# FFN row transposes one slot later, with their splits, the back transposes, the additions, the store and the next row load

## Chip, cores and metric

The kernel runs on one core of a Trainium2 chip. The metric is device time in microseconds (us) of that core, lower is better. Before the change the median of three runs is 2927.73 us (2926.43 to 2928.63).

## What is computed

One layer of a network on `x` of 16 x 1024 rows of 256 float32 numbers: a graph attention block with its residual, then a feed-forward block (FFN) of eight experts with its residual. The change touches only the FFN:

```python
x = x + _L0_gnn_ref(_layernorm(x), adj, W, a)
x = x + _L0_ffn_ref(_layernorm(x), Wr, br, W1, b1, ..., Wo, bo)

def _L0_ffn_ref(x, ...):
    w = softmax(mean(x, axis=0) @ Wr + br)
    h = relu(bn(einsum('bfd,edh->bfeh', x, W1) + b1))
    h = relu(bn(einsum('bfeh,ehk->bfek', h, W2) + b2))
    y = einsum('bfeh,ehd->bfed', h, Wo) + bo
    return einsum('bfed,fe->bfd', y, w)
```

The gate `w` weighs the eight experts for each of the 1024 row places, from the mean over the 16 batches.

## The kernel before

The attention stage fills the first 715 us or so of the span and is not touched. The FFN stage (`ffn_block`) works on 32 tiles of 512 rows. Each tile goes through eight experts, so there are 256 steps. The work of all engines is written out by hand as one loop of slots: in slot `u` each engine does its part for several steps at once, and `tile_due(u, at, ahead)` says that a once-per-tile job is due in the slot whose place in the tile is `at` (0 to 7), for the tile `ahead` of the current one. "Slot 3" below means a slot with `u % 8 == 3`. Engines run their queues in order and meet at semaphores only.

Per slot, in the order of each queue:

- TensorE (`slot`, from L1040): the layer 2 products of step u+2 (12 matmuls of 512 columns, `z_layer(1, ...)`, read `h1_hi`, `h1_lo`, shown as `z_ps<-h_hi`); then the once-per-tile transposes; then the output products of step u (`y_layer`, 21 matmuls of 256 columns into `m_ps`, L1019 to L1022); then the layer 1 products of step u+4 (12 matmuls, shown as `z_ps<-xT_hi`). Every float32 product is made of three matmuls (`split_matmul`, L52 to L54) from an upper and a lower part of each operand.
- ScalarE (from L1173): second half of a layer 1 activation, two halves of the layer 2 activation of step u+2, upper part `h1_hi` (L1185), first half of the next layer 1 activation (all activations are L1149), the once-per-tile upper parts `xT_hi` (L1124), the upper part `h2_hi` of the layer 2 sums (L1163), and in slot 0 the normalised rows `xn` of the next tile (`normalise`, L1131, four instructions).
- VectorE (from L1259): once-per-tile work first, then the lower part `h2_lo` (L1287), the gating multiply (L1294), the lower part `h1_lo` (L1299), three sums (L1304, L1307, L1310).
- SyncE issues DMAs: the operand `wo_ops` of the next step, once per tile the store of finished rows and the load of rows two tiles ahead, and the gate row. GpSimd finishes the row statistics in slot 6.

The three PSUM banks of `z_ps` are shared: the first layer 1 product of a slot writes the bank that the second half of the layer 2 product of the same slot used, so it waits for ScalarE to have read that (`relu2_ready`). Layer 2 products wait for `h1_lo`.

Once per tile, before the change: slot 0 ScalarE normalises the next tile; slots 1 and 2 TensorE transposes its rows (`transpose_x`, L994, four transposes into the one bank `turn_ps`) and ScalarE takes the upper parts; slots 2 and 3 VectorE takes the lower parts `xT_lo` (`lower_x`, L1227); slots 3 and 4 TensorE transposes the previous tile's output back (`transpose_y`, L1002, same bank); slots 4 and 5 VectorE adds that to the rows (`add_out`, L1232) and adds the bias table to the next tile's rows (`residual`, L1239); slot 6 SyncE stores the rows, VectorE starts statistics (L73). The transposed rows are first read in slot 4, by the layer 1 products at the end of TensorE's slot.

Of the kernel before, what the change touches and what calls it, by code (L numbers as in the profile page):

```python
# [37 lines left out]
def wait(eng, sem, value):  # L38

    if isinstance(value, int) and value <= 0:  # L40
        return
    eng.wait_ge(sem, value)


def bits(ap):

    return ap.bitcast(FP32)
# [749 lines left out]
def ffn_block(nc, B, Wo, x1_dram, w_dram, wo_dram, out, ident, minus_half, node_table, w12_hi, w12_lo,  # L797
# [20 lines left out]
    with ctx:  # L818
# [54 lines left out]
        def is_step(s):  # L873
            return 0 <= s < NS

        def tile_due(u, at, ahead):

            t = u // E + ahead
            return t if u % E == at and 0 <= t < TILES else None
# [3 lines left out]
        @block.sync  # L883
        def _(sp):
            def load_sums(e):
                for m in range(KB):
                    sp.dma_start(wo_sums[e % 2][:, (1 - m):4:2, :],
                                 Wo[e].rearrange("(k p) d -> p k d", p=P)[:, :, m * P:(m + 1) * P]) \
                        .then_inc(sums_in[e % 2], DMA)

            def load_gate(s):
                sp.dma_start(gate[s % 2][:, :], w_dram[s % E, (s // E) % CH].partition_broadcast(P)) \
                    .then_inc(gate_in[s % 2], DMA)

            def load_x1(t):
                sp.dma_start(x1_sb[t % XB][:, :, :], x1_dram[t % CH, t // CH]).then_inc(x1_in[t % XB], DMA)

            def rows_out(t):
                return out[t // CH].rearrange("(c s p) d -> c p s d", c=CH, p=P)[t % CH]

            def slot(u):
                e = u + 1
                if 0 <= e < E:

                    sp.wait_ge(S["wo_lo_ready"], e + 1)
                    sp.dma_start(wo_dram[e], bits(wo_ops[e % 2][:, :, :, :])).then_inc(ops_stored[e % 2], DMA)
                    if e + 2 < E:
                        load_sums(e + 2)
                s = u + 1
                if E <= s < NS:  # L910

                    sp.wait_ge(S["step_done"], s - 1)
                    if s < E + 2:
                        sp.wait_ge(ops_stored[s % 2], DMA * (E // 2))
                    sp.dma_start(bits(wo_ops[s % 2][:, :, :, :]), wo_dram[s % E]).then_inc(ops_in[s % 2], DMA)
                t = tile_due(u, 6, -1)
                if t is not None:
                    sp.wait_ge(S["out_ready"], 2 * (t + 1))
                    sp.dma_start(rows_out(t), x1_sb[t % XB][:, :, :]).then_inc(stored[t % XB], DMA)
                t = tile_due(u, 0, 2)  # L920
                if t is not None:
                    wait(sp, stored[t % XB], DMA * (t // XB))
                    load_x1(t)
                s = u + Z2 + 2
                if u >= -Z2 and s < NS:

                    sp.wait_ge(S["gated_ready"], s - 1)
                    load_gate(s)

            for e in range(2):  # L930
                load_sums(e)
            load_x1(1)
            sp.wait_ge(S["wT_ready"], 1)
            sp.dma_start(w_dram.rearrange("e c n -> e (c n)"), wT_sb).then_inc(w_stored, DMA)
            sp.wait_ge(w_stored, DMA)
            for s in range(2):
                load_gate(s)
            for u in range(-Z1, NS):
                slot(u)
            t = TILES - 1  # L940
            for i, h in enumerate((1, 0)):
                rows = slice(h * CT // 2, (h + 1) * CT // 2)
                sp.wait_ge(S["out_ready"], 2 * t + (i + 1))
                sp.dma_start(rows_out(t)[:, rows, :], x1_sb[t % XB][:, rows, :]).then_inc(stored[t % XB], DMA)
            for i in range(XB):
                sp.wait_ge(stored[i], DMA * (TILES // XB + (1 if i == t % XB else 0)))
            for i in range(2):
                sp.wait_ge(ops_stored[i], DMA * (E // 2))
# [41 lines left out]
        def _(pe):  # L990
# [49 lines left out]
            def slot(u):  # L1040
                s = u + Z2
                if is_step(s):
                    pe.wait_ge(S["h1_lo_ready"], s + 1)
                    wait(pe, S["relu2_ready"], 2 * s - 1)
                    z_layer(1, s % E, 0, h1_hi[s % 2], h1_lo[s % 2])

                    if is_step(s + 1):
                        pe.wait_ge(S["h1_ready"], 2 * (s + 1) + 1)
                    else:
                        pe.wait_ge(S["relu2_ready"], 2 * s)  # L1050
                    z_layer(1, s % E, 1, h1_hi[s % 2], h1_lo[s % 2])
                if u == -2:
                    transpose_gate()
                if u == -1:
                    gate_bias()
                for d in range(KB):
                    t = tile_due(u, 1 + d, 1)
                    if t is not None and u >= 0:
                        pe.wait_ge(norm.xn_ready, t + 1)
                        if d == 0:  # L1060
                            wait(pe, S["out_ready"], 2 * (t - 2))
                        else:
                            pe.wait_ge(S["xT_lo_ready"], 2 * t + 1)
                        transpose_x(turn, d)
                for h in range(2):
                    t = tile_due(u, 3 + h, -1)
                    if t is not None:
                        pe.wait_ge(S["comb_ready"], COMBINES * (t + 1))
                        if h == 0:
                            wait(pe, S["xT_lo_ready"], 2 * min(t + 3, TILES))  # L1070
                        else:
                            pe.wait_ge(S["out_ready"], 2 * t + 1)
                        transpose_y(turn, h)
                s = u
                if is_step(s):
                    pe.wait_ge(S["h2_lo_ready"], s + 1)
                    if s < E:
                        pe.wait_ge(S["wo_lo_ready"], s + 1)
                    else:
                        pe.wait_ge(ops_in[s % 2], DMA * (s // 2 - E // 2 + 1))  # L1080
                    if s == 0:
                        pe.wait_ge(S["table_ready"], 1)
                    elif s % E == 0:
                        pe.wait_ge(S["prod_ready"], 2 * (s // E))
                    y_layer(s % E, wo_ops[s % 2], h2_hi[s % 2], h2_lo[s % 2])
                s = u + Z1
                if is_step(s):
                    i = (s // E) % 2
                    if s % E == 0:
                        pe.wait_ge(S["xT_lo_ready"], 2 * (s // E + 1))  # L1090
                    wait(pe, S["relu2_ready"], 2 * (s - 1))
                    wait(pe, S["h1_ready"], 2 * (s - 1) + 1)
                    z_layer(0, s % E, 0, xT_hi[i], xT_lo[i])
                    wait(pe, S["h1_ready"], 2 * s)
                    z_layer(0, s % E, 1, xT_hi[i], xT_lo[i])
# [17 lines left out]
            for u in range(1 - Z1, NS):  # L1113
                slot(u)
# [6 lines left out]
        def _(act):  # L1121
# [51 lines left out]
            def slot(u):  # L1173
# [17 lines left out]
                t = tile_due(u, E - 1, 0)  # L1191
# [3 lines left out]
                    act.activation(prod[:, 0:4, :].rearrange("p q c -> p (q c)"),  # L1195
                                   m_ps[:, 0:2, :].rearrange("p k c -> p (k c)"), ACT.Copy).then_inc(S["prod_ready"], 1)
                for d in range(KB):
                    t = tile_due(u, 1 + d, 1)
                    if t is not None and u >= 0:
                        upper_x(turn, t, d)  # L1200
                second_upper(u + Z2)
                t = tile_due(u, 0, 1)
# [17 lines left out]
            for u in range(1 - Z1, NS):  # L1220
                slot(u)

        @block.vector
        def _(dve):
# [34 lines left out]
            def slot(u):  # L1259
# [6 lines left out]
                for i in range(2):  # L1266
                    t = tile_due(u, i, -1)
                    if t is not None:
                        combine(t, i)
                    t = tile_due(u, 2 + i, 1)  # L1270
                    if t is not None and u >= 0:
                        lower_x(turn, t, i)
                    t = tile_due(u, 4 + i, -1)
                    if t is not None:
                        dve.wait_ge(S["out_psum"], 2 * t + (i + 1))
                        add_out(turn, t, i)
                    t = tile_due(u, 4 + i, 1)
                    if t is not None and u >= 0:
                        residual(t, i)
                t = tile_due(u, 6, 2)  # L1280
# [31 lines left out]
                t = tile_due(u, 6, 2)  # L1312
                if t is not None:
                    norm.mean_var(dve, t + 1, False)
                t = tile_due(u, E - 1, 0)
# [40 lines left out]
            t = TILES - 1  # L1356
# [44 lines left out]
```

## Time and profile before

| | value |
|---|---|
| median of 3 runs | 2927.73 us |
| profiled execution | 2927.11 us |
| its span, first to last instruction | 2925.3 us |
| mean granted TensorE clock | 0.993 of full |
| TensorE matmul busy | 2812.7 us (96%) |
| VectorE busy | 2414.9 us (83%) |
| ScalarE busy | 2141.2 us (73%) |
| HBM traffic over the span | 151 GB/s |

The span leaves 1.8 us of the profiled execution outside it. Busy time is an average over the whole program; ends of matmuls are modelled, so TensorE's gaps are best read from the starts of instructions.

### The profile page before, as it was taken

What the parts mean: (1) busy time and instruction counts of PE and PEld (TensorE: products, weight loads), DVE (VectorE), ACT (ScalarE), POOL (GpSimd) and SP (SyncE); (2) the same over time, 40 slices, a digit from 0 to 9 for tenths busy, and PEclk for the clock granted to TensorE, in tenths of its full rate; (3) what the DMA queues carried; (4) which work ended last, traced back from release to release, by engine and by line L of the source; (5) the groups of instructions that cost most, each with busy time, mean ns of one, the idle gap of its engine ahead of it and who ended that gap; (6) DMA issues with size and microseconds to landing.
All of it is one profiled execution on the core that took longest, in us unless ns stands there. A gap on an engine that the chain in (4) does not pass through costs nothing.

```text
span 2925.3 us, 48929 instructions
## 1 busy us (share of the span) xinstructions
PE 2812.7 (96%) x17110; PEld 2478.9 (85%) x17110; DVE 2414.9 (83%) x3528; ACT 2141.2 (73%) x3035; POOL 703.6 (24%) x985
## 2 busy tenths in 40 slices
PE   7999999998889999999999999999999999999998
PEld 7989899998678888888888888888888888888887
DVE  7999999996678888888888888888888888888887
ACT  6889888887666676677776676677677777677665
POOL 5888888887100000000000000000000000000000
PEclk9999999999999999999999999999999999999999
DMA  4444444442445455545455445455455445445544
GB/s 145 155 158 152 151 158 151 148 154 93 124 147 156 151 165 159 150 164 160 146 159 160 150 156 160 147 165 160 153 160 160 148 157 161 152 153 161 150 156 136
DMA packets 159980, 445.25 MB, mean 152 GB/s; under 512 B 16016, under 2 KB 73784, under 8 KB 159808
## 3 DMA queue, kind: packets, MB, share of 16 engines
q1 hardware_dynamic: 159808, 442.96, 48.5%
q8 instruction: 108, 1.77, 0.2%
q14 instruction: 64, 0.52, 0.1%
HBM read 401.97 MB, written 40.93 MB: 151 GB/s over the span
## 4 chain that ended last, share of the span: by engine, by line
PE 70%; ACT 3%; DVE 2%; issue 1%; DMA 0%; ACTq 0%; DVEq 0%
PE z_ps L52 16%; PE z_ps L53 16%; PE z_ps L54 16%; PE m_ps L1019 7%; PE m_ps L1021 7%; PE m_ps L1022 7%; ACT ffn_xn L1131 2%; PE turn_ps L994 1%; PE turn_ps L1002 1%; DVE h_lo L1287 1%; DVE h_sums L1294 0%; DVE h_lo L1299 0%; ACT wo_ops L1170 0%; ACT h_hi L1163 0%; PE m_ps L1036 0%
## 5 line engine op out<-in xcount | busy, mean ns | idle before, releaser
L1149 ACT ACTIVATE h<-z_ps,bn_shift,bn_scale 128x512 f32<-128x512 f32 x1024 | 755.7, 775 | 615.0 <-PE z_ps L54 580.3
L1287 DVE TENSOR_TENSOR h_lo<-h_sums,h_hi 128x1792 fp32r<-128x1792 f32 x256 | 518.5, 2026 | 205.6 <-ACT h_hi L1163 202.4
L1019 PE MATMUL m_ps<-h_hi,wo_ops 128*128 128x256 f32 x1792 | 514.5, 287 | 4.0 <-DVE h_lo L1287 4.0
L1022 PE MATMUL m_ps<-h_hi,wo_ops 128*128 128x256 f32 x1792 | 503.9, 281 | 0.0
L1021 PE MATMUL m_ps<-h_lo,wo_ops 128*128 128x256 f32 x1792 | 503.6, 281 | 0.0
L1163 ACT ACTIVATE h_hi<-h_sums 128x1792 fp32r<-128x1792 f32 x256 | 435.4, 1701 | 43.7 <-DVE h_sums L1310 34.0
L86 POOL TENSOR_TENSOR ffn_vareps<-ffn_mv,ln_eps 128x4 f32<-128x4 f32 x32 | 6.4, 199 | 1888.5 <-DVE ffn_mv L80 1888.5
L1294 DVE TENSOR_TENSOR h_sums<-h,gate_row 128x1024 f32<-128x1024 f32 x256 | 313.8, 1226 | 146.9 <-ACT h L1149 127.0
L52 PE MATMUL z_ps<-h_hi,w_hi 128*128 128x512 f32 x1024 | 406.4, 397 | 12.0 <-DVE h_lo L1299 12.0
L52 PE MATMUL z_ps<-xT_hi,w_hi 128*128 128x512 f32 x1024 | 406.6, 397 | 2.3 <-ACT h L1149 1.4
L53 PE MATMUL z_ps<-xT_lo,w_hi 128*128 128x512 f32 x1024 | 405.5, 396 | 0.0
L53 PE MATMUL z_ps<-h_lo,w_hi 128*128 128x512 f32 x1024 | 405.4, 396 | 0.0
L54 PE MATMUL z_ps<-xT_hi,w_lo 128*128 128x512 f32 x1024 | 405.4, 396 | 0.0
L54 PE MATMUL z_ps<-h_hi,w_lo 128*128 128x512 f32 x1024 | 404.8, 395 | 0.0
L1019 PEld LDWEIGHTS m_ps<-h_hi,wo_ops 128*128 128x128 f32 x1792 | 339.4, 189 | 9.9 <-DVE h_lo L1287 4.2
L1021 PEld LDWEIGHTS m_ps<-h_lo,wo_ops 128*128 128x128 f32 x1792 | 339.4, 189 | 5.5
L1022 PEld LDWEIGHTS m_ps<-h_hi,wo_ops 128*128 128x128 f32 x1792 | 338.7, 189 | 0.0
L1299 DVE TENSOR_TENSOR h_lo<-h,h_hi 128x1024 fp32r<-128x1024 f32 x256 | 312.1, 1219 | 1.0 <-ACT h_hi L1185 1.0
L52 PE MATMUL attn_ps<-wh_hi,pT_hi 128*128 128x256 f32 x1024 | 306.5, 299 | 0.0
L53 PE MATMUL attn_ps<-wh_lo,pT_hi 128*128 128x256 f32 x1024 | 289.7, 283 | 0.0
L54 PE MATMUL attn_ps<-wh_hi,pT_lo 128*128 128x256 f32 x1024 | 289.6, 283 | 0.0
L1185 ACT ACTIVATE h_hi<-h 128x1024 fp32r<-128x1024 f32 x256 | 270.3, 1056 | 0.0
(149 smaller groups left out, 5485.4 us busy)
## 6 DMA issues: line engine op xcount, KB each, us to landing
wo_ops<-wo_scratch SPq DMA_DIRECT2D x248, 896.0 KB, 6.4
adj_sb<-in_adj SPq DMA_DIRECT2D x128, 512.0 KB, 3.5
gate_row<-w_scratch SPq DMA_DIRECT2D x256, 256.0 KB, 4.6
x_sb<-in_x SPq DMA_DIRECT2D x64, 256.0 KB, 2.8
x_scratch<-x_sb SPq DMA_DIRECT2D x128, 128.0 KB, 1.8
ffn_x<-x_scratch SPq DMA_DIRECT2D x32, 512.0 KB, 7.8
out<-ffn_x SPq DMA_DIRECT2D x31, 512.0 KB, 8.0
wo_scratch<-wo_ops SPq DMA_DIRECT2D x8, 896.0 KB, 4.2
```

The lines of the kernel that those rows point to most:

```text
L52: pe.matmul(out, w_hi, x_hi, start=first, stop=False)
L53: pe.matmul(out, w_hi, x_lo, start=False, stop=False)
L54: return pe.matmul(out, w_lo, x_hi, start=False, stop=last)
L1019: pe.matmul(m_at(q), w_hi, x_hi[:, x, :], start=e == 0 and q in OPENERS, stop=False, skip_group_check=True)
L1021: pe.matmul(m_at(q), w_hi, x_lo[:, x, :], start=False, stop=False, skip_group_check=True)
L1022: done = pe.matmul(m_at(q), w_lo, x_hi[:, x, :], start=False, stop=e == E - 1, skip_group_check=True)
L1149: return act.activation(dst, src, ACT.Relu, bias=bn_shift[layer][:, col], scale=bn_scale[layer][:, col])
L1163: act.activation(h2_hi[s % 2][:, :, :], g2[:, 1:8, :], ACT.Copy).then_inc(S["h2_hi_ready"], 1)
L1185: act.activation(h1_hi[s % 2][:, :, :], h1[:, :, :], ACT.Copy).then_inc(S["h1_hi_ready"], 1)
L1287: dve.tensor_tensor(h2_lo[s % 2][:, :, :], g2[:, 1:8, :], bits(h2_hi[s % 2][:, :, :]), ALU.subtract) \
L1294: dve.tensor_tensor(h2_rows, h2[:, :, :], gate[s % 2][:, :].unsqueeze(1).to_broadcast([P, KB, BANK]), ALU.mult).then_inc(S["gated_ready"], 1)
L1299: dve.tensor_tensor(h1_lo[s % 2][:, :, :], h1[:, :, :], bits(h1_hi[s % 2][:, :, :]), ALU.subtract) \
```

## The change

Ten once-per-tile jobs get another slot. The two groups of row transposes go from slots 1 and 2 to 2 and 3, with ScalarE's upper parts; VectorE's lower parts from 2 and 3 to 3 and 4; the back transposes from 3 and 4 to 4 and 5; the additions of the output from 4 and 5 to 5 and 6; the store from 6 to 7; the load of the rows two tiles ahead from 0 to 1. The addition of the bias table goes the other way, from slots 4 and 5 to 2 and 3. No instruction is added or removed, and every semaphore wait keeps its value. Slot 0's normalisation, slot 6's statistics and the copies of the products in slot 7 stay.

```diff
@@ SyncE, slot @@
-                t = tile_due(u, 6, -1)
+                t = tile_due(u, 7, -1)
                 if t is not None:
                     sp.wait_ge(S["out_ready"], 2 * (t + 1))
                     sp.dma_start(rows_out(t), x1_sb[t % XB][:, :, :]).then_inc(stored[t % XB], DMA)
-                t = tile_due(u, 0, 2)
+                t = tile_due(u, 1, 2)
@@ TensorE, slot @@
                 for d in range(KB):
-                    t = tile_due(u, 1 + d, 1)
+                    t = tile_due(u, 2 + d, 1)
...
                 for h in range(2):
-                    t = tile_due(u, 3 + h, -1)
+                    t = tile_due(u, 4 + h, -1)
@@ ScalarE, slot @@
                 for d in range(KB):
-                    t = tile_due(u, 1 + d, 1)
+                    t = tile_due(u, 2 + d, 1)
                     if t is not None and u >= 0:
                         upper_x(turn, t, d)
@@ VectorE, slot @@
-                    t = tile_due(u, 2 + i, 1)
+                    t = tile_due(u, 3 + i, 1)
                     if t is not None and u >= 0:
                         lower_x(turn, t, i)
-                    t = tile_due(u, 4 + i, -1)
+                    t = tile_due(u, 5 + i, -1)
                     if t is not None:
                         dve.wait_ge(S["out_psum"], 2 * t + (i + 1))
                         add_out(turn, t, i)
-                    t = tile_due(u, 4 + i, 1)
+                    t = tile_due(u, 2 + i, 1)
                     if t is not None and u >= 0:
                         residual(t, i)
```

## Rows read from the trace of the kernel before

**Rows 1.** The page: TensorE's busy time, share of the span, instructions

```profile
PE 2812.7 (96%) x17110; PEld 2478.9 (85%) x17110; DVE 2414.9 (83%) x3528; ACT 2141.2 (73%) x3035; POOL 703.6 (24%) x985
```

**Rows 2.** TensorE's waits in the whole span: us in total, times, longest

```profile
PE turn_ps L994 <- ACT ffn_xn L1131: 31.0, 31, 2.3
...
PE z_ps L52 <- DVE h_lo L1299: 12.0, 8, 6.3
```

**Rows 3.** Busy time in one stretch: length, engines, granted clock, DMA share, GB/s

```profile
1000.00:1500.00 500.00, 493.34 (x2789) 425.37 (x2788) 409.87 (x497) 351.33 (x407) 24.22 (x35) 1.00 0.50 156
```

**Rows 4.** TensorE in time, slots 0 to 4: start, duration, engine, line, [idle before]

```profile
1782.83 0.39 PE L52 MATMUL z_ps<-h_hi,w_hi 128*128 128x512 f32 x1
...
1790.89 0.39 PE L52 MATMUL z_ps<-h_hi,w_hi 128*128 128x512 f32 x1
...
1794.75 0.66 PE L994 MATMUL turn_ps<-ident,ffn_xn 128*128 128x128 f32 x4 [0.90 <-ACT ffn_xn L1131]
...
1797.71 0.39 PE L52 MATMUL z_ps<-xT_hi,w_hi 128*128 128x512 f32 x1
...
1800.51 0.39 PE L52 MATMUL z_ps<-h_hi,w_hi 128*128 128x512 f32 x1
...
1809.01 0.39 PE L52 MATMUL z_ps<-h_hi,w_hi 128*128 128x512 f32 x1
...
1817.54 0.40 PE L52 MATMUL z_ps<-h_hi,w_hi 128*128 128x512 f32 x1
```

**Rows 5.** ScalarE in time, slots 0 to 2 of the same tile

```profile
1791.03 1.71 ACT L1163 ACTIVATE h_hi<-h_sums 128x1792 fp32r<-128x1792 f32 x1 [0.55 <-DVE h_sums L1310]
1792.63 2.06 ACT L1131 ACTIVATE ffn_xn<-ffn_x,ffn_shift,ffn_rstd 128x256 f32<-128x256 f32 x4
1794.60 2.09 ACT L1149 ACTIVATE h<-z_ps,bn_shift,bn_scale 128x512 f32<-128x512 f32 x3
...
1802.31 2.10 ACT L1149 ACTIVATE h<-z_ps,bn_shift,bn_scale 128x512 f32<-128x512 f32 x3
```

**Rows 6.** VectorE in time, slots 1, 2 and 3 of the same tile

```profile
1796.79 1.23 DVE L1294 TENSOR_TENSOR h_sums<-h,gate_row 128x1024 f32<-128x1024 f32 x1 [1.99 <-ACT h L1149]
1797.93 1.22 DVE L1299 TENSOR_TENSOR h_lo<-h,h_hi 128x1024 fp32r<-128x1024 f32 x1
...
1805.74 1.22 DVE L1299 TENSOR_TENSOR h_lo<-h,h_hi 128x1024 fp32r<-128x1024 f32 x1
...
1809.12 0.69 DVE L1227 TENSOR_TENSOR xT_lo<-turn_ps,xT_hi 128x512 fp32r<-128x512 f32 x1 [0.63 <-ACT xT_hi L1124]
1810.71 2.03 DVE L1287 TENSOR_TENSOR h_lo<-h_sums,h_hi 128x1792 fp32r<-128x1792 f32 x1 [0.90 <-ACT h_hi L1163]
```

**Rows 7.** VectorE in slot 7, before the tile's chain starts

```profile
1778.64 1.23 DVE L1294 TENSOR_TENSOR h_sums<-h,gate_row 128x1024 f32<-128x1024 f32 x1 [0.37 <-ACT h L1149]
```

**Rows 8.** ScalarE in the first tile, ahead of a waiting layer 1 product

```profile
811.85 2.10 ACT L1149 ACTIVATE h<-z_ps,bn_shift,bn_scale 128x512 f32<-128x512 f32 x3
```

**Rows 9.** TensorE there: two products that waited

```profile
781.18 0.66 PE L994 MATMUL turn_ps<-ident,ffn_xn 128*128 128x128 f32 x2 [2.99 <-DVE xT_lo L1227]
...
814.01 0.50 PE L52 MATMUL z_ps<-xT_hi,w_hi 128*128 128x512 f32 x1 [0.86 <-ACT h L1149]
814.35 0.39 PE L53 MATMUL z_ps<-xT_lo,w_hi 128*128 128x512 f32 x1
814.57 0.40 PE L54 MATMUL z_ps<-xT_hi,w_lo 128*128 128x512 f32 x1
```

**Rows 10.** VectorE in slots 4 and 6: additions, statistics, and what follows

```profile
1816.69 0.68 DVE L1232 TENSOR_TENSOR ffn_x<-turn_ps,ffn_x 128x512 f32<-128x512 f32 x1
...
1833.74 1.40 DVE L73 BATCH_NORM_STATS2 ffn_stats<-ffn_x 128x6 f32<-128x256 f32 x4
1835.60 2.03 DVE L1287 TENSOR_TENSOR h_lo<-h_sums,h_hi 128x1792 fp32r<-128x1792 f32 x1 [0.46 <-ACT h_hi L1163]
1837.99 1.23 DVE L1294 TENSOR_TENSOR h_sums<-h,gate_row 128x1024 f32<-128x1024 f32 x1 [0.37 <-ACT h L1149]
```

**Rows 11.** DMA issues: engine, op, times, KB each, median us to landing

```profile
wo_ops<-wo_scratch SPq DMA_DIRECT2D x248, 896.0 KB, 6.4
...
out<-ffn_x SPq DMA_DIRECT2D x31, 512.0 KB, 8.0
```

**Rows 12.** The chain that ended last, at the tail: start, us, what

```profile
2897.15 0.25 PE z_ps L54
2897.43 0.79 ACT h L1149
2898.30 1.23 DVE h_sums L1294
```

## The prediction

> **What bounds the kernel now.** I read the page's busy line first: TensorE is busy 96% of the span [rows 1], so time is what TensorE spends plus the gaps in its queue. The busy times of one stretch of the FFN stage come next: in 500 us TensorE is busy 493, VectorE 410, ScalarE 351, the granted clock is 1.00, the level of 2.4 GHz, and the DMA engines are half idle [rows 3]. So a shift of work between the other engines counts only where TensorE waits for it. The list of TensorE's waits shows one that comes once for each of the 31 tiles that are transposed inside the loop: the first row transpose waits for the last normalised rows of ScalarE, 31.0 us in 31 times [rows 2]. No other wait has that regularity.
>
> Then I read one tile in time, by the start of the first layer 2 product of each slot [rows 4]. Slot 0 runs from 1782.83 to 1790.89, 8.06 us: no transposes, no wait. Slot 2 takes 1809.01 - 1800.51 = 8.50 and slot 3 takes 1817.54 - 1809.01 = 8.53: one group of four transposes costs 0.44 to 0.47. Slot 1 takes 1800.51 - 1790.89 = 9.62, that is 8.06 + 0.45 + 1.11. The 1.11 is the price of the wait as starts tell it; the 0.90 printed beside the transpose is less, because the end of the matmul before is modelled. Of the 30 tiles after the first, 27 give 9.62 to 9.64 for slot 1, and every slot with a group of transposes 8.50 to 8.54.
>
> **What the change does to slot 1.** The transposes leave slot 1, so their wait is gone: normalised rows are there at 1792.63 + 2.06 = 1794.69 [rows 5], and the new place is in slot 2, after 1802. Had nothing else been late, slot 1 would take 8.06 and its last part, the layer 1 products, would start where it does in any plain slot: the layer 1 products precede the next slot by 1800.51 - 1797.71 = 2.80 [rows 4], so 8.06 - 2.80 = 5.26 after the slot's start, at 1790.89 + 5.26 = 1796.15.
>
> What is late next: that product reuses the bank of the layer 2 product of the same slot, and waits until ScalarE has read it. ScalarE's queue in slots 0 and 1 is back to back: upper part of the sums at 1791.03, held by VectorE, normalisation at 1792.63, three activations from 1794.60, which end at 1794.60 + 2.09 = 1796.69 [rows 5]. The third is the one waited for. Before the change TensorE came to it at 1797.71, 1.02 late, and the wait was covered by the stall on the transposes. Now TensorE comes at 1796.15 and waits for 1796.69. Nothing in this chain follows TensorE's progress in slot 1: what feeds 1791.03 is VectorE's queue, which TensorE last held at the gating in slot 7, through an activation [rows 7], and slots 7 and 0 do not change.
>
> The hand-over: in the first tile the same product waited for the same three activations. They ended at 811.85 + 2.10 = 813.95 [rows 8] and the product started at 814.01, 0.06 later; its second matmul came 0.34 after the first, where an undisturbed one comes after 0.22 to 0.23 [rows 9]. So a restart costs 0.11 more. Slot 1 now: product at 1796.69 + 0.06 = 1796.75, next slot at 1796.75 + 2.80 + 0.11 = 1799.66. Slot 1 takes 8.77 instead of 9.62: 0.85 less. The next product needs the lower part of the hidden rows, done at 1797.93 + 1.22 = 1799.15 [rows 6]: in time by 0.5. So this second wait stays hidden, just.
>
> The Trainium skill, "TensorE: Matmul & The Clock Gate", section "Step-by-step: what each phase is for", says that TensorE can pull a weight load ahead of matmuls in flight into a background buffer. If that also worked across a semaphore wait, the restart would cost nothing and the result would be 30 x 0.11 = 3 us lower; the first tile's rows speak against it.
>
> **What moves in, slots 2 to 5.** Four groups of transposes per tile stay four, but they now lie in slots 2, 3, 4, 5 instead of 1 to 4. The group in slot 5 lengthens it by 0.47, as it did slot 3. Net per tile: 0.85 - 0.47 = 0.38.
>
> The other steps I cost at nothing, with their cover:
> - Slot 2, VectorE: an addition of 0.68 (the length of an addition in [rows 10]) stands where a lower part of 0.69 stood; it waits for nothing. Layer 2 products of slot 3 now start 0.85 earlier, near 1808.2, and need the hidden rows' lower part at 1805.74 + 1.22 = 1806.96 [rows 6]: cover 1.2. The activations of slot 2 start at 1802.31 [rows 5], queued behind the upper part and not released by TensorE, so they don't come earlier either; layer 1 products in slot 2 start near 1805.4, after their end at 1804.41: cover 1.0.
> - Slot 3, VectorE: lower part, then an addition, ahead of the long lower part L1287. Before, 1809.12 + 0.69 = 1809.81 and then 0.90 idle until 1810.71 [rows 6]. The addition's 0.68 fits in the 0.90.
> - Slot 4: a lower part for two additions; slot 5: one addition for two. Less than before.
> - Slot 6, VectorE: an addition of 0.68 ahead of the statistics of 1.40 [rows 10]. The idle times behind are 0.46 and 0.37, together 0.83, so the gating, which an activation releases, still starts in time. Behind this queue stand the gating and the lower part of the hidden rows, for which TensorE waits; the latter has the cover of more than a microsecond that slot 1 showed (1.36 between 1799.15 and 1800.51).
> - Back transposes in slots 4 and 5 wait for the lower parts and for the first addition, each one slot behind as before; bank `turn_ps` is handed on in the same order.
> - SyncE: store in slot 7 instead of 6, load in slot 1 instead of 0. The store takes 8.0 us and the operand load 6.4 [rows 11]; an operand load is needed more than a slot (8 us) after its issue, the loaded rows five slots later, and the buffer that was stored is loaded into two slots later, as before. What is queued behind the moved DMAs are the gate row, used two slots later, and the next operand load. The moved load shares its slot with one operand load and one gate row as it did before. Bounds: nothing below, since no wait of TensorE ends on a DMA here; above, a microsecond in 30 tiles if a landing were late, which I don't expect.
>
> **First tile and tail.** In the first tile VectorE also splits the weights, and its queue is the bound. There the second transposes waited 2.99 us for a lower part [rows 9]; now they wait a slot later, and I follow the queues to about 1.1 us less, between 0.3 more and 2.9 less. At the tail the last tile has no row transposes, and the chain that ends last passes through the last layer 2 product of slot 4 [rows 12] and then through ScalarE and VectorE. Of the two groups of back transposes ahead of it one now lies behind it, and not on the chain: 0.47 less.
>
> **The sum.** 30 tiles x 0.38 = 11.4, first tile 1.1, tail 0.5: 13.0 us off a span of 2925.3, which gives 2912.3, and with the 1.8 us around it 2914.1. The profiled execution lies 0.6 below the median of the runs, so on their scale 2914.7.
>
> **Rivals.** (a) Nothing takes the place of the removed wait: slot 1 takes 8.06, each tile saves 1.56 - 0.47 = 1.09, together 30 x 1.09 + 1.6 = 34 us, 2893.5. That is what the list of waits promises. It would need ScalarE's third activation to end by 1796.1 where it ends at 1796.69, and that is 0.6 away in every tile. 6%.
> (b) Slot 2 starts as late as before: if the lower part of the hidden rows, done at 1799.15 [rows 6], came later, since the packed slot 6 leaves VectorE a backlog that runs through slots 7 and 0 into the queue that holds ScalarE at 1791.03, the moved group would be pure cost. At a delay of 0.8 slot 2 starts at 1800.0, slot 1 saves 0.47, and the group in slot 5 takes it back: no gain. From there on the kernel is slower. At 1.36, the whole cover of before, each tile is some 0.5 longer: 30 x 0.5 less 1.6 is 13 us more, 2941. For it: VectorE gets 0.68 more in slot 6, where 0.83 is spare. Against it: slot 7 has an idle 0.37 of its own ahead of the gating [rows 7]. 8%.
> (c) The wait moves as in my forecast, but a second small one of 0.1 to 0.4 us appears, at slot 2's start (0.5 spare) or behind slot 3's addition (0.22 spare): 3 to 12 us more than forecast, 2918 to 2927. 16%. The forecast itself (2909 to 2919) has 70%.
> That the change leaves the stall is no case: the rows are ready 8 us before the new place.
>
> **Range and chances.** The range goes from 2907 (30 x 0.11 for a free restart and 1.8 for the first tile at its best, with a little to spare) to 2923, into (c); (a), (b) and the rest of (c) are left out. A measurement of this kernel can tell about 0.2% from no change, 5.9 us: faster is below 2921.9. Faster 0.82 (the forecast, (a), a third of (c)), same 0.12 (the rest of (c), the start of (b)), slower 0.06.
>
> **What would show it.** In the profile after: no wait of L994 on L1131 outside the first tile; in its stead some 30 waits of a layer 1 product on ScalarE's L1149, printed at 0.3 to 0.4 us each (0.2 less than starts tell); slot 1 near 8.77, slots 2 to 5 near 8.5, the others 8.06. If slot 1 is 8.06, (a) holds; if slot 2 starts with a wait for L1299, (b) or (c). The prediction is wrong if ScalarE's three activations in slot 1 don't start right behind the normalisation, or if slot 6 or 7 shows a new wait of TensorE.

## The result: 2914.57 us, and the profile after

The changed kernel takes 2914.57 us (median of five, 2912.28 to 2915.3) against 2927.64 us before (median of five): a ratio of 0.9956, 95% interval 0.9941 to 0.997. Run again beside other kernels it gave 2915.63 us, 0.9958 (0.9945 to 0.9971). The forecast was 2914.7. All medians and ranges are of fast executions: one execution of a kernel below (only the load undone) took 8441.29 us where its five others took 2913 to 2916, and it is left out.

The page of the profile after, its first lines; TensorE does the same work in a span 12.5 us shorter (busy line of [rows 1]):

```profile
span 2912.8 us, 48929 instructions
## 1 busy us (share of the span) xinstructions
PE 2816.4 (97%) x17110; PEld 2482.6 (85%) x17110; DVE 2411.8 (83%) x3528; ACT 2136.5 (73%) x3035; POOL 703.9 (24%) x985
```

TensorE's waits in the whole span after (us in total, times, longest):

```profile
PE z_ps L52 <- ACT h L1149: 18.2, 34, 1.7
...
PE z_ps L52 <- DVE h_lo L1299: 11.6, 7, 6.3
...
PE turn_ps L994 <- DVE xT_lo L1227: 3.1, 1, 3.1
```

The 31 waits of the transposes on L1131 of [rows 2] are gone. In their place stand 34 waits of a layer product on ScalarE's activations, 18.2 us, where there had been 2 of them with 1.4 us (too small a group for the lists above). Of the 34, 30 are the first layer 1 product of slot 1, once in each tile after the first; 4 lie in the first tile. The wait on `h_lo` is nearly as long as it was (11.6 and 12.0 us).

TensorE in time after, one tile, to be laid beside [rows 4]: the first layer 2 product of slots 0 and 1; the first layer 1 product of slot 1 with its weight load (PEld) and the matmul behind it; then the first layer 2 product of slots 2 to 6:

```profile
1778.07 0.39 PE L52 MATMUL z_ps<-h_hi,w_hi 128*128 128x512 f32 x1
...
1786.13 0.39 PE L52 MATMUL z_ps<-h_hi,w_hi 128*128 128x512 f32 x1
...
1791.98 0.19 PEld L52 LDWEIGHTS z_ps<-xT_hi,w_hi 128*128 128x128 f32 x1 [0.64 <-ACT h L1149]
1791.98 0.50 PE L52 MATMUL z_ps<-xT_hi,w_hi 128*128 128x512 f32 x1 [0.44 <-ACT h L1149]
1792.32 0.39 PE L53 MATMUL z_ps<-xT_lo,w_hi 128*128 128x512 f32 x1
...
1794.88 0.40 PE L52 MATMUL z_ps<-h_hi,w_hi 128*128 128x512 f32 x1
...
1803.42 0.39 PE L52 MATMUL z_ps<-h_hi,w_hi 128*128 128x512 f32 x1
...
1811.92 0.39 PE L52 MATMUL z_ps<-h_hi,w_hi 128*128 128x512 f32 x1
...
1820.45 0.40 PE L52 MATMUL z_ps<-h_hi,w_hi 128*128 128x512 f32 x1
...
1828.98 0.39 PE L52 MATMUL z_ps<-h_hi,w_hi 128*128 128x512 f32 x1
```

Slot 0 takes 8.06, slot 1 takes 1794.88 - 1786.13 = 8.75 (it was 9.62), slots 2 to 5 take 8.54, 8.50, 8.53 and 8.53. ScalarE over the same slots, to be laid beside [rows 5]:

```profile
1786.27 1.71 ACT L1163 ACTIVATE h_hi<-h_sums 128x1792 fp32r<-128x1792 f32 x1 [0.56 <-DVE h_sums L1310]
1787.88 2.06 ACT L1131 ACTIVATE ffn_xn<-ffn_x,ffn_shift,ffn_rstd 128x256 f32<-128x256 f32 x4
1789.85 2.09 ACT L1149 ACTIVATE h<-z_ps,bn_shift,bn_scale 128x512 f32<-128x512 f32 x3
```

The three activations end at 1789.85 + 2.09 = 1791.94, and the layer 1 product starts at 1791.98. ScalarE's own times against the start of slot 1 did not move: the activations begin 1789.85 - 1786.13 = 3.72 after it, and 1794.60 - 1790.89 = 3.71 before. What moved is where TensorE waits for them.

| slot of the tile, median of 28 or 29 tiles | 0 | 1 | 2 | 3 | 4 | 5 | 6 | 7 | mean of a tile |
|---|---|---|---|---|---|---|---|---|---|
| before | 8.06 | 9.62 | 8.50 | 8.52 | 8.54 | 8.05 | 8.06 | 8.06 | 67.44 |
| after | 8.06 | 8.76 | 8.54 | 8.50 | 8.52 | 8.53 | 8.05 | 8.06 | 67.03 |

### The profile page after: what moved, and what is told of

It reads as the page before. It is cut to its first block, busy times and chain, and to the rows that moved or that the text cites. A ratio compares the mean times of both kernels' runs of the same rounds, so it can differ in the third digit from the quotient of the medians.

```text
span 2912.8 us, 48929 instructions
## 1 busy us (share of the span) xinstructions
PE 2816.4 (97%) x17110; PEld 2482.6 (85%) x17110; DVE 2411.8 (83%) x3528; ACT 2136.5 (73%) x3035; POOL 703.9 (24%) x985
## 4 chain that ended last, share of the span: by engine, by line
PE 68%; ACT 4%; DVE 1%; issue 1%; DMA 0%; ACTq 0%; DVEq 0%
PE z_ps L52 16%; PE z_ps L54 16%; PE z_ps L53 16%; PE m_ps L1019 6%; PE m_ps L1021 6%; PE m_ps L1022 6%; ACT h L1149 2%; ACT ffn_xn L1131 2%; PE turn_ps L994 1%; PE turn_ps L1002 1%; DVE h_lo L1287 0%; DVE h_sums L1294 0%; DVE h_lo L1299 0%; ACT wo_ops L1170 0%; PE m_ps L1036 0%
## 5 line engine op out<-in xcount | busy, mean ns | idle before, releaser
L1287 DVE TENSOR_TENSOR h_lo<-h_sums,h_hi 128x1792 fp32r<-128x1792 f32 x256 | 518.5, 2025 | 205.8 <-ACT h_hi L1163 200.7
L1163 ACT ACTIVATE h_hi<-h_sums 128x1792 fp32r<-128x1792 f32 x256 | 435.0, 1699 | 61.5 <-DVE h_sums L1310 59.6
L52 PE MATMUL z_ps<-xT_hi,w_hi 128*128 128x512 f32 x1024 | 410.4, 401 | 18.2 <-ACT h L1149 18.2
L52 PE MATMUL z_ps<-h_hi,w_hi 128*128 128x512 f32 x1024 | 406.0, 396 | 11.6 <-DVE h_lo L1299 11.6
```

Source lines behind the costliest of these rows:

```text
L52: pe.matmul(out, w_hi, x_hi, start=first, stop=False)
L1163: act.activation(h2_hi[s % 2][:, :, :], g2[:, 1:8, :], ACT.Copy).then_inc(S["h2_hi_ready"], 1)
L1287: dve.tensor_tensor(h2_lo[s % 2][:, :, :], g2[:, 1:8, :], bits(h2_hi[s % 2][:, :, :]), ALU.subtract) \
```

## The experiments

**Gauge and test of the cause: a fifth activation.** If ScalarE's queue behind the normalisation sets the end of slot 1 in both kernels, more work there costs both the same.

```diff
                 wait(act, S["xT_psum"], 2 * t)
+                act.activation(spare[:, :], x1_sb[t % XB][:, 0, :], ACT.Identity,
+                               bias=shift[:, 0:1], scale=norm.rstd[:, 0:1])
                 for s in range(CT):
```

> The kernel before with a fifth activation of 128x256 ahead of the four of the normalisation, written to a buffer that nobody reads: it lengthens the row that TensorE waited for by 0.49 us (2.06 for four, started 0.49 apart). Both theories agree here, it is the gauge: the first row transpose waits 0.49 longer in each tile, 31 x 0.49 = 15 us more than before, about 2942.8.

> The changed kernel with the same fifth activation. My theory, that slot 1 of the changed kernel ends by ScalarE's third activation behind the normalisation: slot 1 grows from 8.76 to 9.25, 15 us more than the changed kernel, about 2929.5. Rival, that the wait of the changed kernel has another cause (TensorE's own progress or VectorE): ScalarE's extra 0.49 is hidden and the time stays near 2914.6.

Measured: 2944.82 us for the kernel before with it (ratio 1.0055, 1.0038 to 1.0071), 2931.17 us for the changed one (1.0010 of before, 1.0001 to 1.0020). Slot 1 grew from 9.62 to 10.12 and from 8.76 to 9.25: 0.50 and 0.49. The time grew by 16.5 us for the kernel before (2928.29 in the executions beside it) and by 16.6 for the changed one, where 15 were expected. The product that waits in the changed kernel with it (its lines are three further down):

```profile
1799.16 0.50 PE L52 MATMUL z_ps<-xT_hi,w_hi 128*128 128x512 f32 x1 [0.93 <-ACT h L1152]
```

The wait is 0.93 where it was 0.44. So the extra work lands on TensorE whole, and the rival that it is hidden falls.

**The cause shortened, in the changed kernel.**

```diff
-                for s in range(CT):
+                for s in range(1):
                     last = act.activation(norm.xn[:, s, :], x1_sb[t % XB][:, s, :], ACT.Identity,
```

> The changed kernel with one of the four activations of the normalisation: rows 128 to 511 of each tile keep the numbers of the first tile, left out on purpose to shorten the cause by 1.47 us. My theory: the moved wait (0.70 a tile with its restart) vanishes, slot 1 takes 8.06, 30 x 0.70 = 21 us less than the changed kernel, about 2893.5, and nothing else takes its place. Rival, that another wait is right behind (the lower part of the hidden rows at slot 2, with 0.5 of cover by the trace, if it doesn't move with ScalarE): slot 1 stays above 8.2 and the gain is under 15 us.

Measured: 2892.64 us (0.9879, 0.9862 to 0.9895). Slot 1 takes 8.06, a tile 66.29. With the cause gone nothing else waits in its place.

**The same cause moved, in the kernel before.** All transposes stay where they were; ScalarE normalises earlier in slot 0.

```diff
                     act.activation(h1_hi[s % 2][:, :, :], h1[:, :, :], ACT.Copy).then_inc(S["h1_hi_ready"], 1)
+                t = tile_due(u, 0, 1)
+                if t is not None and u >= 0:
+                    normalise(t)
...
                 second_upper(u + Z2)
-                t = tile_due(u, 0, 1)
-                if t is not None and u >= 0:
-                    normalise(t)
```

> The kernel before, all transposes in their old slots, with the whole normalisation moved ahead in ScalarE's queue within slot 0, right behind the upper part h1_hi, where ScalarE is idle 1.8 us. My theory, that place and length of the normalisation are the whole cause: the rows are ready some 3 us earlier, no wait on the transposes and none behind it, slot 1 takes 8.06 + 0.45 = 8.51, 31 x 1.11 = 34 us less than before, about 2893. Rival, that the transposes in slot 1 themselves are too early (or the normalisation in the new place delays the activation of the next layer 1 product): some of the wait stays, and the time is at or above the changed kernel's 2914.6.

Measured: 2892.15 us (0.9877, 0.9860 to 0.9893), with everything computed. ScalarE in slot 0 and the start of slot 1 of this kernel:

```profile
1769.96 1.08 ACT L1185 ACTIVATE h_hi<-h 128x1024 fp32r<-128x1024 f32 x1
1770.91 2.09 ACT L1131 ACTIVATE ffn_xn<-ffn_x,ffn_shift,ffn_rstd 128x256 f32<-128x256 f32 x4
1772.88 0.79 ACT L1149 ACTIVATE h<-z_ps,bn_shift,bn_scale 128x512 f32<-128x512 f32 x1
1774.19 1.71 ACT L1163 ACTIVATE h_hi<-h_sums 128x1792 fp32r<-128x1792 f32 x1 [0.52 <-DVE h_sums L1310]
1775.80 2.10 ACT L1149 ACTIVATE h<-z_ps,bn_shift,bn_scale 128x512 f32<-128x512 f32 x3
```

and TensorE's transposes in its slot 1:

```profile
1776.85 0.60 PE L994 MATMUL turn_ps<-ident,ffn_xn 128*128 128x128 f32 x4
```

The normalisation fills idle time of ScalarE: the upper part L1163 is still held by VectorE (0.52 idle before it, 0.55 in [rows 5]), so it starts no later. The transposes have no wait, and slot 1 takes 8.53: 8.06 and a group of transposes. This version beats both kernels and needs none of the ten moves. The Trainium skill, "TensorE: Matmul & The Clock Gate", section "Architectural detail: the array is 16× 32×32, not 1× 128×128", has ScalarE's queue as strictly first in, first out. The trace agrees: in the kernel before, ScalarE stood idle for 0.55 us ahead of L1163 [rows 5] while the normalisation was queued behind it, whose rows were there, since here it runs before L1163. So the place in the queue counts as much as the length.

**What the changed kernel allows: normalisation in slot 1.** The edit above on the changed kernel, but with `tile_due(u, 1, 1)` ahead of `normalise(t)`.

> The changed kernel with the whole normalisation moved into slot 1 behind the upper part h1_hi, which only the later transposes make possible. My theory: ScalarE has idle time there until the sums of VectorE end, the moved wait before the layer 1 products is gone, slot 1 takes 8.06, each tile 66.3 instead of 67.03: 21 us less than the changed kernel, about 2893.5. Rival: the 2.06 us push the upper part h2_hi and the activations of slot 2 back by a microsecond or more, and layer 1 products in slot 2 wait in their turn: 2900 to 2915.

Measured: 2892.06 us (0.9876, 0.9860 to 0.9893). ScalarE in slots 1 and 2:

```profile
1779.93 2.07 ACT L1131 ACTIVATE ffn_xn<-ffn_x,ffn_shift,ffn_rstd 128x256 f32<-128x256 f32 x4
1782.11 0.78 ACT L1149 ACTIVATE h<-z_ps,bn_shift,bn_scale 128x512 f32<-128x512 f32 x1
1783.20 1.70 ACT L1163 ACTIVATE h_hi<-h_sums 128x1792 fp32r<-128x1792 f32 x1 [0.31 <-DVE h_sums L1310]
```

VectorE still holds L1163 (0.31 idle), so the 2.07 us cost TensorE nothing. Three ways to take the normalisation away from slot 1's activations end at the same 66.29 a tile: this is eight slots of 8.06 and four groups of transposes at 0.44 to 0.48, with no wait of TensorE in the tile.

**The wait filled instead of removed.**

```diff
@@ TensorE @@
-                    t = tile_due(u, 4 + h, -1)
+                    t = tile_due(u, (1, 4)[h], -1)
@@ VectorE @@
-                    t = tile_due(u, 5 + i, -1)
+                    t = tile_due(u, (2, 5)[i], -1)
```

(with the waits for the bank `turn_ps` renumbered to the new order).

> The changed kernel with the first group of back transposes in slot 1 instead of slot 4, and the second in slot 4 instead of 5, with their additions. The wait in slot 1 stays where it is but 0.47 us of transposes stand in it. My theory: slot 1 keeps 8.76, since ScalarE sets its end, slot 5 falls from 8.53 to 8.06: 30 x 0.47 = 14 us less than the changed kernel, about 2901. Rival, that a wait is not filled by work put ahead of it (the transposes come on top): slot 1 takes 9.2 and the time stays at 2914.6.

Measured: 2901.17 us (0.9906, 0.9889 to 0.9922). Slot 1 takes 8.76, slot 5 8.05, a tile 66.62. ScalarE's activations and TensorE's product in slot 1:

```profile
1784.13 2.10 ACT L1151 ACTIVATE h<-z_ps,bn_shift,bn_scale 128x512 f32<-128x512 f32 x3
```

```profile
1786.28 0.50 PE L52 MATMUL z_ps<-xT_hi,w_hi 128*128 128x512 f32 x1
```

No gap is printed, yet the product starts right behind the activations' end at 1784.13 + 2.10 = 1786.23 and takes the 0.50 of a restart. The slot is as long as without the transposes in it: they stand in the wait.

**The rows made late again.** Two activations of the normalisation stay at the end of slot 0, two go to the end of slot 1.

```diff
-                t = tile_due(u, 0, 1)
-                if t is not None and u >= 0:
-                    normalise(t)
+                for i, rows in enumerate((range(2), range(2, CT))):
+                    t = tile_due(u, i, 1)
+                    if t is not None and u >= 0:
+                        normalise(t, rows)
```

> The changed kernel with two of the four activations of the normalisation at the end of slot 0 and two at the end of slot 1, behind the upper part h2_hi. Worked out from the changed kernel's rows: the moved wait of slot 1 goes (8.06 instead of 8.76), but the second half ends some 11.5 us after slot 1's start, while the row transposes of slot 2 come at 10.9, so a wait of TensorE on the normalised rows is back, 0.65 a tile, now in slot 2 (9.2 instead of 8.54): 2912 to 2914.5, nothing won. Rival, that the new place of the transposes makes them safe from any such wait: the whole 0.70 a tile is won, 2893.

Measured: 2917.41 us (0.9963, 0.9949 to 0.9978), 3 us above the upper end of what was expected. Slot 1 takes 8.06 as foretold, slot 2 takes 9.27 instead of the 9.2 worked out, a tile 67.12. The first row transpose in slot 2:

```profile
1798.58 0.44 PE L994 MATMUL turn_ps<-ident,ffn_xn 128*128 128x128 f32 x2 [0.54 <-ACT ffn_xn L1132]
```

The wait of before is back in the new place. The move of the transposes buys time only against rows made in slot 0; it is no cure by itself.

**VectorE's packed slot 6, packed more.**

```diff
-                    t = tile_due(u, 2 + i, 1)
+                    t = tile_due(u, 6, 1)
                     if t is not None and u >= 0:
                         residual(t, i)
```

> The changed kernel with both additions of the bias table in slot 6, where VectorE already has an addition and the statistics: 1.2 us more in its most packed slot. Theory of cover: 0.64 idle ahead of the gating, then about 0.2 of ScalarE's and 0.1 of VectorE's in slots 7 and 0 take up all but 0.2 us, which reaches ScalarE's chain into slot 1: 30 x 0.2 = 7 us more than the changed kernel, 2918 to 2925. If the backlog is absorbed whole: 2914.6. If nothing of it is (the rival that ended on the slower side): 30 x 1.2 = 36 more, 2950.

Measured: 2919.99 us (0.9973, 0.9963 to 0.9982). Slot 1 takes 8.85 instead of 8.76, where 0.2 more was expected, and a tile 67.15, 0.12 more. So the time lies in the expected range in part for another reason. Against the first trace of the changed kernel the span is 5.4 us longer: 29 tiles give 3.5, the first two together 2.7 (below), and the stretch before them and the tail took 0.8 less. VectorE in slot 6 and 7 of this kernel:

```profile
1831.70 0.68 DVE L1239 TENSOR_TENSOR ffn_x<-ffn_x,node_table 128x512 f32<-128x512 f32 x1
1832.30 0.68 DVE L1232 TENSOR_TENSOR ffn_x<-turn_ps,ffn_x 128x512 f32<-128x512 f32 x1
1832.90 0.68 DVE L1239 TENSOR_TENSOR ffn_x<-ffn_x,node_table 128x512 f32<-128x512 f32 x1
1833.50 1.40 DVE L73 BATCH_NORM_STATS2 ffn_stats<-ffn_x 128x6 f32<-128x256 f32 x4
1834.82 2.00 DVE L1287 TENSOR_TENSOR h_lo<-h_sums,h_hi 128x1792 fp32r<-128x1792 f32 x1
1836.96 1.23 DVE L1294 TENSOR_TENSOR h_sums<-h,gate_row 128x1024 f32<-128x1024 f32 x1
...
1842.61 2.03 DVE L1287 TENSOR_TENSOR h_lo<-h_sums,h_hi 128x1792 fp32r<-128x1792 f32 x1 [1.48 <-ACT h_hi L1163]
1844.76 1.23 DVE L1294 TENSOR_TENSOR h_sums<-h,gate_row 128x1024 f32<-128x1024 f32 x1
```

The idle time before both gatings (0.37 in slots 6 and 7 before, [rows 7, 10]) is used up, and a tenth of a microsecond goes on into slot 1: ScalarE's L1163 starts 0.23 after the start of slot 1 instead of 0.14 (medians of 27 tiles). So rival (b)'s road exists: a backlog of slot 6 reaches slot 1. But it needs more than the 0.68 that the change put there.

**Two parts costed at nothing, undone.** Together, then each alone, with the changed kernel itself run beside the single ones:

```diff
-                t = tile_due(u, 1, 2)
+                t = tile_due(u, 0, 2)
...
-                    t = tile_due(u, 2 + i, 1)
+                    t = tile_due(u, 4 + i, 1)
                     if t is not None and u >= 0:
                         residual(t, i)
```

> The changed kernel with the additions of the bias table back in slots 4 and 5 and the load of the next rows back in slot 0: two parts of the change undone. My theory, which costs both at nothing: 2914.6 within 1.5 us, all slots the same length. Rival, that the earlier additions or the later load carry some of the gain: 2 us or more above.

> The changed kernel once more, as the gauge for the two runs beside it: 2914.6, slot 1 at 8.76, and the first tile (from the layer 2 products of its slot 1 to those of the next tile's slot 0) in 71.5 us as in its first trace, if that length is a property of the kernel and not of one execution.

> The changed kernel with only the additions of the bias table back in slots 4 and 5. With load and additions undone the later tiles kept their length, but the first tile took 75.6 us instead of 71.5, with the granted clock at 0.72 in 788 to 800 us of the span, where it was 1.00. If the additions' place is what does it: first tile 75.6 again, 2 to 4 us above the run beside it. If the load's place does it or one execution's chance: first tile near 71.5 and no difference.

> The changed kernel with only the load of the next rows back in slot 0. If the additions do it: first tile 71.5, no difference from the run beside it. If the load does it: first tile 75.6, 2 to 4 us above.

| | time, us | range | a later tile | first tile |
|---|---|---|---|---|
| changed kernel, first trace | 2914.57 | 2912.28 to 2915.3 | 67.03 | 71.5 |
| changed kernel, again | 2915.63 | 2915.16 to 2916.2 | 67.04 | 71.6 |
| only the load undone | 2915.2 | 2913.02 to 2916.21 | 67.05 | 72.4 |
| only the additions undone | 2917.28 | 2914.28 to 2918.79 | 67.04 | 75.7 |
| both undone | 2917.42 | 2917.03 to 2918.14 | 67.04 | 75.6 |
| additions in slot 6 | 2919.99 | 2917.55 to 2922.42 | 67.15 | 75.4 |

In the later tiles both parts are free, as I costed them. In the first tile the kernels with late additions take 4 us more, of which the tile after returns 1.3 (75.05 instead of 76.3 from its slot 0 to the next tile's slot 1). The times say 1.7 to 2.8 us, and with the ranges of the single run overlapping, the traces carry this more than the times do. By slots of the first tile, with the granted clock of the stretch behind TensorE's wait for `xT_lo`:

| | slot 3 | clock, 788 to 800 | slot 5 | slot 6 | slot 7 | clock, 831 to 836 | first tile |
|---|---|---|---|---|---|---|---|
| changed kernel | 11.95 | 1.00 | 9.94 | 10.96 | 8.16 | 1.00 | 71.5 |
| only the load undone | 13.46 | 0.86 | 9.94 | 10.96 | 8.17 | 1.00 | 72.4 |
| normalisation in slot 1 | 13.47 | 0.86 | 9.94 | 10.95 | 9.74 | 0.70 | 71.8 |
| only the additions undone | 14.48 | 0.72 | 10.79 | 10.95 | 9.73 | 0.66 | 75.7 |
| additions in slot 6 | 14.45 | 0.72 | 9.94 | 12.16 | 9.71 | 0.68 | 75.4 |

The additions themselves cost 0.85 in slot 5, or 1.20 (two additions) in slot 6. Slots 3 and 7 take 2.5 and 1.6 us more, and they go with the clock; slots 2 and 4 give back 0.7 to 1.3. (With the normalisation in slot 1 the first tile is short all the same, since its slot 1 takes 8.60 instead of 10.66.) The busy times of 787 to 800 us (length, engines, granted clock, DMA share, GB/s), of the changed kernel, with the load undone, and with the additions undone:

```profile
787.00:800.00 13.00, 8.96 (x50) 7.56 (x51) 10.16 (x12) 7.67 (x10) 2.50 (x4) 1.00 0.44 136
```

```profile
787.00:800.00 13.00, 9.54 (x46) 8.28 (x47) 10.06 (x13) 7.17 (x9) 2.87 (x5) 0.87 0.44 132
```

```profile
787.00:800.00 13.00, 10.02 (x45) 8.83 (x44) 8.59 (x10) 6.51 (x9) 4.48 (x8) 0.74 0.39 122
```

The columns are length, then TensorE, its weight loads, VectorE, ScalarE and GpSimd busy, then clock, DMA share and GB/s. With the additions undone TensorE does 45 matmuls in more busy time than the 50 of the changed kernel: part of the stretch runs at 1.2 instead of 2.4 GHz. In all three, TensorE had waited 3.0 to 3.1 us for `xT_lo` a moment before, and ahead of slot 7 it waits 1.8 us for `h_lo` whether the clock falls there or not.

That the additions' place makes the clock fall is not shown. The clock in 788 to 800 is 0.72 in all three traces of the changed kernel with late additions and 0.86 to 1.00 in its eight with early ones. But in slot 7 it falls with early additions too (normalisation in slot 1). And in the three traces with the transposes in their old slots, which all have late additions, the 12 us behind the same wait of 3.0 us have 0.87, 0.86 and 1.00, and the first tile takes 71.0 to 73.9. Why it falls behind one wait and not behind another stays open; no run here holds the wait and varies the rest.

## Why the prediction was right, and where a term was off

- **Slot 1.** Forecast: the wait moves to the layer 1 product, slot 1 at 8.77. Measured 8.75 to 8.76. The hand-over took 0.04 (forecast 0.06), the second matmul came 1792.32 - 1791.98 = 0.34 after the first, the restart I took from [rows 9]. The wait is printed at 0.43 to 0.44 in nearly every tile, a little above the 0.3 to 0.4 that I named as a sign. That the ScalarE row is the cause was an argument in the prediction; the fifth activation, the single one and the two moved normalisations show it.
- **The restart.** The 0.34 (0.33 to 0.34) is there in the waiting product of all 30 tiles, and the product in the filled slot has its 0.50 too. The weight load shows why: in slot 0 of every tile, where nothing waits, it starts 0.11 before its matmul, and in the waiting product it starts with the matmul, at 1791.98. The Trainium skill, "TensorE: Matmul & The Clock Gate", section "Step-by-step: what each phase is for", has weight loads pulled ahead of matmuls in flight. The trace agrees for products that don't wait. The section doesn't say what a semaphore wait does to this; here no load was pulled ahead across one.
- **Slot 5.** 8.05 to 8.53, 0.48, forecast 0.47. Net per tile by the medians 0.38, as forecast; by the means 67.44 - 67.03 = 0.41, so 30 tiles (from 837.28 to 2861.71 before, 838.35 to 2850.37 after) gave 12.4 us instead of 11.4.
- **VectorE's covers.** Both held, and both were wider than my sums. Slot 3: 0.57 idle stays before L1287 where 0.90 - 0.68 = 0.22 was left by the sum. TensorE's slots 2 and 3 start earlier by what slot 1 saved, and the ScalarE and VectorE chain doesn't follow at once: L1287 starts 1805.48 - 1803.42 = 2.06 after the slot's start instead of 1.70. Slot 6: the statistics are followed by L1287 almost without idle time, and 0.64 stays before the gating where the sum left 0.15, so nothing reaches slot 7. VectorE in both, to be laid beside [rows 6, 10]:

```profile
1803.63 0.68 DVE L1227 TENSOR_TENSOR xT_lo<-turn_ps,xT_hi 128x512 fp32r<-128x512 f32 x1
1804.23 0.68 DVE L1239 TENSOR_TENSOR ffn_x<-ffn_x,node_table 128x512 f32<-128x512 f32 x1
1805.48 2.03 DVE L1287 TENSOR_TENSOR h_lo<-h_sums,h_hi 128x1792 fp32r<-128x1792 f32 x1 [0.57 <-ACT h_hi L1163]
...
1828.12 0.68 DVE L1232 TENSOR_TENSOR ffn_x<-turn_ps,ffn_x 128x512 f32<-128x512 f32 x1
1828.72 1.40 DVE L73 BATCH_NORM_STATS2 ffn_stats<-ffn_x 128x6 f32<-128x256 f32 x4
1830.19 2.03 DVE L1287 TENSOR_TENSOR h_lo<-h_sums,h_hi 128x1792 fp32r<-128x1792 f32 x1
1832.85 1.23 DVE L1294 TENSOR_TENSOR h_sums<-h,gate_row 128x1024 f32<-128x1024 f32 x1 [0.64 <-ACT h L1149]
```

- **First tile.** Forecast 1.1 less, bounds 2.9 less to 0.3 more. From its slot 1 to the next slot 0 it took 71.5 us instead of 73.9, 2.4 less. The difference is inside the bounds, but how much of it the change made stays open. The profiled execution of before came to this tile 3.5 us early (see below) and waited longer for its first normalised rows: its slot 1 took 11.75, where the kernel before with a fifth activation, which began at 768.09, took 11.03. Its slot 2 took 13.25 with the granted clock at 0.58 in 781 to 785, and 11.78 in that other kernel at full clock. I had followed the queues at the full clock, and none of this was in the term.
- **Tail.** Forecast 0.47; slot 3 of the last tile went from 8.53 to 8.06. Another 0.7 came behind it, since the last products ran in part at the full clock: granted 0.60 in 2901.0 to 2905.2, where before they had 0.50 in 2912.8 to 2917.7.
- **What the sum didn't have.** The stretch before the first tile, which the change doesn't touch, took 3.5 us more in the profiled execution of after (the first tile's slot 1 began at 766.87 instead of 763.38). In the other traces here it begins at 765 to 768, so the execution of before was the early one: its granted clock was 1.00 in 750 to 758 us, and it was 0.59 in after and 0.57 to 0.68 in the others. The profiled difference is thus 3.5 - 2.4 - 12.4 - 1.2 = -12.5. That it comes so near the forecast 13.0 is luck in part: the tiles, which the mechanism is about, gave 12.4 for 11.4, and what lies outside them came to -0.1 for the forecast -1.6, by terms of up to 3.5 us that cancel.
- **Rivals.** (a) would have needed ScalarE's queue to be earlier; the moved normalisations made it so and gave (a)'s 2893 to a microsecond or two. (b)'s road was shown to be open only beyond what the change loads on it (0.09 in slot 1 for 1.2 us more in slot 6). (c)'s second wait did not appear in the later tiles.

## What to carry to other kernels

When a wait is taken away by moving the waiter, look at what the releaser's queue does next and for whom: here the same ScalarE queue released a second product, which the stall had covered by 1 us, and 0.70 of the 1.11 us of the stall came back there. Compare moving the waiter (13 us here) with moving the work that is waited for within its own in-order queue, into a gap that a third engine sets (36 us, with one edit). A wait that can't be removed can be filled with once-per-tile work (another 13 us here). In a queue written by hand either is a small edit.

## What the runs showed that I had not expected

The first tile of the FFN stage takes 71.0 to 75.7 us in the traces here, and much of the spread goes with the clock that TensorE is granted behind a 3 us wait and behind a 1.8 us wait: granted 1.00, 0.87 and 0.74 in the same 13 us of three kernels that differ only in jobs that TensorE doesn't do. The later tiles repeat to 0.02 us in kernels that differ in nothing that TensorE waits for. So an edit that should be free is best judged by the later tiles, and a difference of one to four microseconds in one trace's first tile is not yet the edit's.
